# Dividing attention by its row sums before the transpose: one whole-bank reciprocal on VectorE in place of a copy, four transposes and a broadcast multiply

## The reference, cut to what matters

```python
Q = split_heads(layernorm(x)) * 32 ** -0.5        # 16 batches, 16 heads of 32, 512 tokens
Kh, Vh = split_heads(k_mem), split_heads(v_mem)
logits = einsum('bhqd,bhkd->bhqk', Q, Kh) + b     # and a mask over the keys
weights = softmax(logits, axis=-1)
out = einsum('bhqk,bhkd->bhqd', weights, Vh)
x = x + tanh(g_xattn) * out
```

## Time and profile before

| | us |
|---|---|
| median of 3 runs (lowest, highest) | 1887.98 (1885.58, 1890.13) |
| the profiled execution, its own time | 1887.81 |
| its span | 1886.1 |
| PE busy | 1729.0 (92%) |
| DVE busy | 1373.5 (73%) |
| POOL busy | 1250.1 (66%) |
| ACT busy | 1191.9 (63%) |

### The profile page before, as it was taken

One profiled execution on the slowest core, in us unless ns is written; L12 is line 12 of the kernel. 1 busy time (PEld: TensorE's weight loads), 2 busy tenths in 40 slices (PEclk: granted clock), 3 DMA queues, 4 the chain that ended last, 5 costly groups with the idle time before them and its releaser, 6 DMA issues. The chain is left out here.

```text
span 1886.1 us, 32941 instructions
## 1 busy us (share of the span) xinstructions
PE 1729.0 (92%) x9696; PEld 1040.0 (55%) x9697; DVE 1373.5 (73%) x2997; ACT 1191.9 (63%) x2052; POOL 1250.1 (66%) x1490
## 2 busy tenths in 40 slices
PE   2699999999999999999999999996399999999997
PEld 1344555555555555555555555543277777777775
DVE  4677887877878788878787888752676676666675
ACT  4267677677676776767767767663365555555554
POOL 1258577576685775766756757562368888888887
PEclk9999999999999999999999999996599999999999
DMA  5979898899898988998989888844278887978784
GB/s 118 171 131 190 156 171 185 127 205 156 156 193 162 171 185 128 205 153 160 194 161 172 184 128 170 131 124 146 70 130 162 151 148 153 168 139 153 149 153 72
DMA packets 173067, 291.45 MB, mean 155 GB/s; under 512 B 37982, under 2 KB 42078, under 8 KB 172944
## 3 DMA queue, kind: packets, MB, share of 16 engines
q1 hardware_dynamic: 138704, 219.88, 60.3%
q0 software_dynamic: 32928, 67.68, 20.4%
q10 hardware_dynamic: 1312, 2.38, 0.8%
HBM read 127.09 MB, written 71.63 MB: 105 GB/s over the span
## 5 line engine op out<-in xcount | busy, mean ns | idle before, releaser
L1066 DVE TENSOR_REDUCE bank<-bank 128x1 f32<-128x512 f32 x1024 | 696.8, 691 | 256.8 <-PE bank L841 248.6
L700 ACT ACTIVATE prob<-bank 128x512 f32<-128x512 f32 x1024 | 592.7, 597 | 356.9 <-PE bank L829 356.0
L619 POOL TENSOR_TENSOR prob<-prob 128x512 f32<-128x512 f32 x256 | 320.3, 1281 | 326.1 <-PE bank L764 326.1
L829 PE MATMUL bank<-stB,stA 100*128 100x512 f32 x1024 | 477.2, 467 | 16.0 <-ACT prob L700 13.6
L841 PE MATMUL bank<-stA,stB 98*128 98x512 f32 x1024 | 423.3, 416 | 35.7 <-DMA stA<-regrouped_then_w 20.3
L829 PEld LDWEIGHTS bank<-stB,stA 100*128 100x128 f32 x1024 | 193.4, 189 | 248.9 <-ACT prob L700 176.4
L623 POOL TENSOR_TENSOR prob<-prob 128x512 f32<-128x512 f32 x256 | 319.5, 1278 | 0.0
L764 PE MATMUL bank<-prob,vin 128*32 128x512 f32 x2048 | 272.7, 605 | 0.7 <-ACT prob L700 0.7
L1332 POOL DMA_INDIRECT out_dram<-yout,scatter_ids x144 | 242.9, 1687 | 45.1 <-issue 41.1
L841 PEld LDWEIGHTS bank<-stA,stB 98*128 98x128 f32 x1024 | 197.8, 193 | 84.4 <-DVE bank L1066 38.9
L1302 POOL DMA_INDIRECT rows_in<-xn_rows,gather_ids x152 | 161.8, 1064 | 86.0 <-DVE rows_in L1517 45.0
(11 more groups left out here) (190 smaller groups left out, 2207.0 us busy)
## 6 DMA issues: line engine op xcount, KB each, us to landing
stB<-regrouped_then_w SPq DMA_DIRECT2D x192, 256.0 KB, 5.8
stA<-regrouped_then_w SPq DMA_DIRECT2D x183, 256.0 KB, 6.7
x_k_then_w<-in_x_dram SPq DMA_DIRECT2D x16, 1024.0 KB, 8.1
x_k_then_w<-in_ctx_dram SPq DMA_DIRECT2D x16, 1024.0 KB, 12.1
vin<-in_ctx_dram SPq DMA_DIRECT2D x16, 1024.0 KB, 9.3
xres<-in_x_dram SPq DMA_DIRECT2D x16, 1024.0 KB, 6.6
out_dram<-xres SPq DMA_DIRECT2D x16, 1024.0 KB, 7.4
xn_rows<-xn SPq DMA_DIRECT2D x64, 256.0 KB, 5.6
```

What stands on the lines that cost most here:

```text
L619: pool.tensor_tensor(first[:, j, :], first[:, j, :], more[:, j, :], ALU.add).then_inc(s_acc, 1)
L700: act.activation(prob_of(st, 0, u)[:, j, :], psS[j % 2][:, :], ACT.Exp).then_inc(s_exp, 1)
L829: pe.matmul(psS[j % 2][:, :], stA[0:100, g, j, kt * P:(kt + 1) * P], stB[0:100, g, j, :], start=True, stop=True).then_inc(s_qk, 1)
L1066: dve.tensor_reduce(mx[:, s // 4, s % 4:s % 4 + 1], psM[s % 2][:, :], AX.X, ALU.max).then_inc(s_mx, 1)
```

## The change

The sums are no longer copied or turned. DVE inverts the whole bank of sums in place (128x512) at `s` 3 and multiplies `attT` by it at `s` 4, before the transpose. The turn `DT`, the tiles `sumT` and `rsum`, ACT's copy of the sums, four transposes, the 128x16 reciprocal and the multiply after the transpose go away. `OT` moves from `s` 9 to `s` 8, `MT` from 5 to 6, ACT's copy of the maxima from 6 to 7, and DVE's `lo_part` of the keys from 5 to 6.

```diff
-TURNS = [("TQ", 3), ("SM", -1), ("TK", 3), ("MT", 1), ("DT", -1), ("OT", -1), ("XT", -5), ("LG", -5)]
+TURNS = [("TQ", 3), ("SM", -1), ("TK", 3), ("MT", 1), ("OT", -1), ("XT", -5), ("LG", -5)]
...
@@ ScalarE
-                        if s == 6 and st.on(1) and st.l >= 0:
+                        if s == 7 and st.on(1) and st.l >= 0:
                             take_maxima(st)
...
-                        if s == 3 and st.on(-1):
-                            if st.l >= 2:
-                                b, before = turn_of(st, "DT", -1)
-                                act.wait_ge(s_turn[b], before + 1)
-                            bank, took = take_turn(act, st, "SM")
-                            act.activation(sumT[:, :], bank[:, :], ACT.Copy).then_inc(took, 1)
...
@@ TensorE
-                        if s == 5 and st.on(1) and st.l >= 0:
+                        if s == 6 and st.on(1) and st.l >= 0:
                             turn_maxima(st)
-                        if s in (7, 9) and st.on(-1):
-                            name, src = ("DT", sumT) if s == 7 else ("OT", attT)
-                            if s == 7:
-                                b, before = turn_of(st, "SM")
-                                pe.wait_ge(s_took[b], before + 1)
-                            else:
-                                pe.wait_ge(s_out, st.count(1, -1, 1))
-                            bank, done = put_turn(pe, st, name)
+                        if s == 8 and st.on(-1):
+
+                            b, before = turn_of(st, "SM")
+                            pe.wait_ge(s_took[b], before + 1)
+                            bank, done = put_turn(pe, st, "OT")
                             for i in range(NT):
-                                last = pe.transpose(bank[:, i * P:(i + 1) * P], src[:, i * P:(i + 1) * P], ident[:, :])
+                                last = pe.transpose(bank[:, i * P:(i + 1) * P], attT[:, i * P:(i + 1) * P], ident[:, :])
                             last.then_inc(done, 1)
...
@@ VectorE
-                        if s in (1, 5) and st.on(3):
-                            lo_part(st, s // 5)
+                        if s in (1, 6) and st.on(3):
+                            lo_part(st, s // 6)
...
-                        if s == 8 and st.on(-1):
-
-                            bank, took = take_turn(dve, st, "DT")
-                            sums = bank[:, :].rearrange("p (i h c) -> p i h c", i=NT, h=HG)[:, :, :, 0]
-                            dve.reciprocal(rsum[:, :, :], sums).then_inc(took, 1)
+                        if s in (3, 4) and st.on(-1):
+
+                            bank, took = take_turn(dve, st, "SM")
+                            if s == 3:
+                                dve.reciprocal(bank[:, :], bank[:, :]).then_inc(s_inv_sum, 1)
+                            else:
+                                dve.wait_ge(s_inv_sum, st.count(1, -1, 1))
+                                dve.wait_ge(s_out, st.count(1, -1, 1))
+                                dve.tensor_tensor(attT[:, :], attT[:, :], bank[:, :], ALU.mult).then_inc(took, 1)
                         if s == 10 and st.on(-1):
-
-                            b, before = turn_of(st, "DT")
-                            dve.wait_ge(s_took[b], before + 1)
-                            i, before = turn_of(st, "OT")
-                            dve.wait_ge(s_turn[i], before + 1)
-                            each = rsum[:, :, :].rearrange("p i (h a) -> p (i h) a", a=1).to_broadcast([P, NT * HG, DH])
-                            heads = psT[i][:, :].rearrange("p (h c) -> p h c", c=DH)
-                            dve.tensor_tensor(heads, heads, each, ALU.mult).then_inc(s_scaled, 1)
-                        if s == 11 and st.on(-1):
                             g, par = st.g(-1), ((st.l - 1) // 4) % 2
```

More of the change, by code:

```diff
@@ L229, in flamingo_kernel @@
             attT = w2a[:, 2 * NT * D + 4 * S:2 * NT * D + 5 * S]
-            sumT = w2a[:, 2 * NT * D + 5 * S:2 * NT * D + 6 * S]
             mT = w2a[0:2 * HG, 2 * NT * D + 6 * S:2 * NT * D + 7 * S].bitcast(F32R)
@@ L247, in flamingo_kernel @@
             place = prob[:, 0, 2, 7 * E:7 * E + 7]
-            rsum = sb("rsum", [P, NT, HG])
             xn2 = sb("xn2", [P, D])
@@ L322, in flamingo_kernel @@
             s_out = sem("attention_copied")
-            s_scaled = sem("attention_scaled")
+            s_inv_sum = sem("sums_inverted")
             s_m = sem("max_logits_ready")
@@ L533, in step @@
                             sp.wait_ge(s_stat, 8 * B)
-                            for name in ("DT", "OT"):
-                                i, before = turn_of(st, name, -1)
-                                sp.wait_ge(s_turn[i], before + 1)
+                            i, before = turn_of(st, "OT", -1)
+                            sp.wait_ge(s_turn[i], before + 1)
                         for e in range(2 * (st.l - (G - 2)), 2 * (st.l - (G - 2)) + 2):
@@ L1095, in step @@
                                 dve.wait_ge(s_res[par], st.bpair(16, -1, 16))
-                            dve.wait_ge(s_scaled, st.count(1, -1, 1))
                             bank, took = take_turn(dve, st, "OT")
```

## The result

The changed kernel takes 2136.02 us (median of 4, 2135.19 to 2137.24) against 1888.75 us on the same chip: 1.1307 of before, 95% interval 1.1291 to 1.1323. That is 247 us lost, where the forecast had 145.7 and a range that ended at 2112 us. The direction was right, the size and the range were not.

A forecast was written before the change was run, and what follows sets the result against it. PE was taken to set the pace. A mean stall of 2.34 us in 61 divisions (142.7 us, PE's saving included) plus 3 us for the last three gave +145.7 on 1887.8: 2033.5 us, range 1985 to 2112.

The forecast's parts named there:

- What bounds it, and what leaves: Attention stage: PE sets the pace; four transposes leave its list, 0.41 us a step; the old and new DVE multiplies cancel.
- The reciprocal's price: DVE's new 512-element reciprocal at sub-step 3: 5.9 ns an element, 3170 ns in all, 3.1 us between starts.
- rival 2: DVE's reciprocal takes 8.3 ns an element, 4.3 us between starts; 2107 us, chance 0.2.
- The stall: PE waits behind DVE's reciprocal in 61 of 64 divisions: mean 2.34 us a step, 142.7 us.
- The delay at sub-step 9: PE's maxima matmul of sub-step 9 starts later: 3.04 us with MAX8, 3.2 with statistics, 2.5 with neither.
- The 0.41 for the turn OT: PE's turn OT moves ahead of sub-step 9, so its 0.41 us is gone from the list behind it.
- without it PE runs at its own pace: Before sub-step 13, with DVE's multiply gone from there, PE stops following DVE and gains 0.35 us.
- the fourth kind: Step with neither MAX8 nor statistics: 2.5 us at sub-step 9, less 0.4 for OT and nothing more, 2.1 us.
- rival 4: PE stands still about 2 us a step and its clock falls in a tenth of the stage: 60 us, 2094 us, chance 0.03.
- Rivals 1 and 3: First: reciprocal at plain rate, 0.65 us between starts, 1863 us, chance 0.08; other: PE recovers part of stall, 1962 us, 0.1.
- Rival 3: PE and DVE decouple again within the step, leaving half of the 2.34 us stall; 1962 us, chance 0.1.
- SP's queue: Placement of the turned maxima's rows waits behind that of the keys' low part; 7.8 us of cover, costed at nothing.

The follow-up runs named there:

- cols16: The changed kernel with its reciprocal cut to the first 16 of the 512 columns of sums, the rest left undivided; 1904.3 us.
- cols256: The changed kernel with only 256 of the 512 columns of sums inverted, the rest left undivided; 1955.5 us.
- cols384: The changed kernel with only 384 of the 512 columns of sums inverted, the rest left undivided; 2038.7 us.
- fill8: The changed kernel, whole, with PE making the logits bank of sub-step 6 eight times, seven of them superfluous; 2049.9 us.
- fill8_res11: The changed kernel with the logits bank of sub-step 6 made eight times and the residual add back at DVE's sub-step 11; 2041.9 us.
- rec_first: The changed kernel with DVE taking the reciprocal ahead of the maximum of sub-step 3 instead of behind it; 2112.7 us.
- pieces: The changed kernel with the reciprocal in four pieces of 128 columns at sub-steps 3 to 6, multiply at 7, OT at 9, turned maxima before the sums; 2186.8 us.
- fill3: The changed kernel with the logits bank of sub-step 6 made three times, two of them superfluous; 2089.2 us.
- old_plus: The kernel before, whole, plus a 512-element DVE reciprocal over a spare 32-row tile at sub-step 3 of 61 steps; 2096.9 us.

## Why the prediction was wrong

**What bounds it, and what leaves.** Right: PE set the pace. Of the worth of the four transposes, 0.41 us in each of 61 steps, cols16 shows 14 of 25 us.

**The reciprocal's price.** Right: 3353 ns for 3170, by a slope of 6.25 ns an element where two short rows had 5.9. The reading of the Trainium skill, "VectorE: DVE Perf Modes", section "First, the fixed hardware budget", as 8.3 ns an element doesn't hold in cols256 and cols384; rival 2 fell with it.

**The stall.** Nearly right: 161.6 us by fill8 against 145.7, and a step of 21.6 us against 21.5. In fill8's MAX8 step the maximum of 3 starts at 706.94 and L834 of sub-step 9 at 714.97, 8.03 us; before it was 708.26 to 713.36, 5.10. The delay is 2.93 us where the working had 3.04. (Two small errors nearly cancel in it: the slot is 3.26 us and not 3.10, and the two masks of 0.20 run behind the low part and not in front of it.) The steps by kind, from one maximum of 3 to the next, means of 13 steps each in the two traces:

| step | before, us | fill8, us | longer by | forecast |
|---|---|---|---|---|
| with statistics (two in four) | 18.62 | 21.61 | 2.98 | 2.5 |
| with MAX8 | 19.17 | 21.42 | 2.25 | 2.28 |
| with neither | 19.31 | 21.81 | 2.50 | 2.1 |
| mean | 18.93 | 21.61 | 2.68 | 2.34 |

The delay at sub-step 9 was right in all kinds (3.06 on average for 2.99). The 0.41 for the turn OT came too, as 0.30 to 0.40. The term that failed in size comes after it: "without it PE runs at its own pace", 0.35 us gained before sub-step 13. The multiply did leave that place, but the residual add moved into it, from 11 to 10, as the diff says; I had taken the add to stay behind the maximum. In the steps with statistics the gain is missing to the end, and fill8_res11 gives 0.34 of it back in them, 8 us in all. In the MAX8 step it is missing before sub-step 13 as well, and the forecast of 2.28 holds only because PE gains as much at the end of the step, which the working did not have: luck. The 0.4 us in the fourth kind was not followed further.

**The clock: the step that failed.** It was rival 4, at a chance of 0.03 and 60 us, and it was added to the sum as nothing. I compared a whole step's busy share (18.5 of 21.5 us) with long stretches before. But PE's gap isn't spread over a step: it stands in one place, and in the 5.20 us up to the fall PE was busy only 3.43. The clock fell once in each step, and that made 86 us (fill8), the whole distance between 2050 and 2136. With that price beside the stall the sum would have been 2120. The stall alone leaves 2050, inside the forecast's own range of 2003 to 2064.

**Rivals 1 and 3.** Neither happened. Rival 3 would have left 1.17 us a step; at full clock 2.68 are left, so PE does not recover. Taking the reciprocal earlier (rec_first) gave 0.4 us a step, moving it behind sub-step 9 or cutting it nothing. SP's queue, costed at nothing, cost nothing: no DMA stands among the waits from 500 to 1200 us.

## What to carry to other kernels

A long instruction on an engine that frees two buffers for another costs nearly its whole length in every round, however idle that engine is on average. Here the mean step took 18.75, 20.08 and 21.61 us in cols16, cols256 and fill8: 1.3 us more for the first 1.50 us of length, 1.5 for the next 1.60. Look at where the idle time lies, before or behind the instruction. Where such a stall hits PE, ask for a second price: look at PE around the gap and not at its share of the round, and take the time at the lower clock. Each microsecond there cost 0.29 us in the changed kernel, 0.32 in pieces, 0.34 in fill3, 0.36 in rec_first and 0.40 in old_plus (how much earlier attention ends in the run with the gap filled, over "low"). A quick test for it is to fill the gap with superfluous matmuls into a bank that is being made anyway.

## What the hardware showed that I had not expected

- The clock fell after a single gap of 1.8 to 2.4 us in each of 61 steps, and as well behind a row of gaps of 0.74, 0.66 and 1.27 us, in a stretch of 6.8 us in which PE was busy 4.1; it came back by itself within the same step. A gap of such length did not bring it down every time: old_plus has 60 over 1.5 us and 32 falls.
- One run of superfluous work (2.1 us of matmuls a step) made a kernel 86 us faster.
- The reciprocal takes 6.25 ns an element: 0.95, 1.76, 2.56, 3.35 us at 128, 256, 384, 512 elements, and for 512 elements on 32 rows in SBUF 3.34 us (old_plus), so neither the rows nor the bank made a difference.
